# A window-attention block and a deformable convolution in one kernel: ScalarE's two-step work split within a slot, with semaphores of its own, and a tile's turns and matmul one slot later

## The chip, the cores and the metric

The kernel runs on one core of one Trainium2 chip. The metric is the device time of one execution in microseconds (us); smaller is better. The engines are TensorE (PE, its weight loads PEld), VectorE (DVE), ScalarE (ACT), GpSimd (POOL) and SyncE (SP), which issues the DMAs here. Each works through its own program in order and meets the others only at semaphores.

## The reference

The input is 16 images of 128 channels and 56x56 pixels. Two layers run one after the other. Cut to what matters:

```python
# layer 0, per image
x = x + dwconv3x3(x)
q, k, v = layernorm(x) @ qkv_w + qkv_b           # 7x7 windows of 8x8 pixels
idx = top_k(mean_q @ mean_k, 4)                   # each window picks 4 windows
o = softmax(q . k[idx] * scale) @ v[idx]          # 49 windows, 4 heads
x = x + (o + dwconv5x5(v)) @ wo                   # the 5x5 one is "lepe"
x = x + mlp(layernorm(x))                         # 128 -> 384, gelu, 384 -> 128
# layer 1, per image
off = relu(conv1x1([relu(conv1x1(gated x)), 2 * feat_up]))
dy, dx, m = conv3x3(off)                          # 8 groups x 9 taps = 72 samples a pixel
out = relu(sum over 72 samples of bilinear(feat_up at (y+dy, x+dx)) * sigmoid(m) @ w_dcn) + x
```

The bilinear sample is computed without a gather. Its weight in a row or a column is the hat max(0, 1 - |distance|), so a column hat times the map is a matmul, and the row hats are multiplied in and summed afterwards.

## The kernel before, in words

Work is cut into **slots**. An image has 28 tiles of two rows and 9 slots q = 0 to 8 in each tile, so 252 slots n. Every engine has a `body(xi, di)` that walks these 252 slots with two images at once: layer 0 of image `xi` and, beside it, the deformable part of the image before, `di`. `body(0, None)` opens, 15 bodies have both (one for image 1, 14 in a hardware loop), and `body(None, 15)` closes with the deformable part alone. In a slot, the order of the calls is the order in which the engine does the work; nothing reorders it.

**The deformable part in a slot.** PE computes `windows` (L956, 32 matmuls) from `hats` and `fx`; DVE multiplies by the row weights in `weigh` (L1473), two slots of PSUM banks ahead at most; POOL adds rows once in three slots (`add_rows`, L634, L636, L639). ACT turns the column distances that a DMA has spread over `hats` into hats, one quarter buffer in each slot and three slots ahead of the matmuls that use them: `column_hats` (L1165 to L1167) is Abs, a drain, then Relu of 1 - x. Once a tile come, for the tile two ahead: the 18 matmuls of `offsets` in slot 0 (L926), `outside` on ACT in slot 1 (L1177 to L1179), `turn_columns` on PE and `copy_columns` on ACT in slot 2 (L933, L1172), and the sigmoid of the masks, `masks`, on ACT in slot 3 (Exp, drain, Ln, drain, Exp, L1184 to L1188). For the tile one ahead ACT makes the row hats in slot `WYH` = 2 (`row_hats`, Abs, drain, Relu, L1193 to L1195). For the tile before, PE turns the samples in the slots `VT` = 3, 4, 6 (`turn_samples`, L969, which waits for POOL's `general`, L722), ACT copies each turn out in the same slot (`copy_samples`, L1200, into `valt`), and in slot `WD` = 7 PE does `deform`, the 18 matmuls of L977, and ACT the `relu` behind it (L1206). POOL's `finish` (L646) waits for that.

**Layer 0 in a slot.** `x_slot` (ACT, DVE) and `x_first` and `x_rest` (PE) hold it. Slots 0 to 26 do the 3x3 convolution on DVE, 9 to 51 the q, k, v projections, 59 to 205 the attention, 81 to 216 the projections and the MLP of the 7 bands (`post`, steps k = 0 to 9, one band every 21 slots), 225 to 238 the offset features. Attention has one window each three slots. In the first (q = 2, 5 or 8) PE computes `scores` (L848), DVE the maxima (L1390) and ACT two Exp (`exps`, L1117); in the second (q = 0, 3 or 6) PE turns the result (L857) and ACT copies it (`copy_turned`, L1123, tile `pt`); in the third (q = 1, 4 or 7) PE does `pv` (L865) and DVE scales the heads (L1397, L1403, tile `osb`). The next `scores` waits for that, because all of it shares one PSUM bank. DVE also has one or two of the 25 taps of `lepe` (L1418) in nearly every slot from 62 to 207, ahead of the scaling.

On ACT a slot is: `column_hats`; then `outside`, `copy_columns`, `row_hats`, `masks`, `copy_samples` or `relu` where the slot has one; then `x_slot`. On PE it is: `windows`, `x_first` (scores or pv), `offsets`, `turn_columns`, `turn_samples` or `deform`, then `x_rest` (the steps of `post` and, behind them, the turn of the scores).

Of the kernel before, what the change touches and what calls it, by code (L numbers as in the profile page):

```python
# [34 lines left out]
CP = 4  # L35
# [19 lines left out]
OM, PXT, VT, WD, WYH = 0, 2, (3, 4, 6), 7, 2  # L55
# [81 lines left out]
def build(nc, a, out):  # L137
# [9 lines left out]
    with ExitStack() as ctx:  # L147
# [162 lines left out]
        s_hb = [sem(f"columns_spread{s}") for s in range(HR)]  # L310
        s_hat = sem("column_hats_ready")
# [729 lines left out]
        def _(act):  # L1041
# [119 lines left out]

            def column_hats(i, n, c):
                act.wait_ge(s_hb[n % HR], cnt(i, 32 * NT * NG // HR, 32 * (n // HR + 1)))
                v = hats[:, n % HR, c * CP:(c + 1) * CP, :].rearrange("p j n -> p (j n)")
                act.activation(v, v, ACT.Abs, bias=const("xneg"))  # L1165
                act.drain()  # L1166
                act.activation(v, v, ACT.Relu, scale=-1.0, bias=1.0).then_inc(s_hat, 1)  # L1167
# [6 lines left out]
            def outside(i, t):  # L1174
                act.wait_ge(s_pxy, cnt(i, NT, t + 1))
                wait(act, s_fm, cnt(i, NT, t))
                act.activation(tmpf[:], pxy[t % 4][:, 0:S], ACT.Abs, bias=const("mid"))  # L1177
                act.drain()
                act.activation(tmpf[:], tmpf[:], ACT.Relu, bias=const("mid"), accum_out=vmx[:]).then_inc(s_vm, 1)  # L1179

            def masks(i, t):
                m = pxy[t % 4][:, 2 * S:3 * S]
                act.wait_ge(s_cl, cnt(i, NT, t + 1))
                act.activation(m, m, ACT.Exp, scale=-1.0)  # L1184
                act.drain()
                act.activation(m, m, ACT.Ln, bias=1.0)
                act.drain()
                act.activation(m, m, ACT.Exp, scale=-1.0).then_inc(s_msk, 1)  # L1188

            def row_hats(i, t):  # L1190
                v = wy[t % 2][:].rearrange("p s r -> p (s r)")
                act.wait_ge(s_wa, cnt(i, NT, t + 1))
                act.activation(v, v, ACT.Abs)  # L1193
                act.drain()
# [33 lines left out]
            def body(xi, di):  # L1228
                for t in range(NT):
# [4 lines left out]
                    for q in range(Q):  # L1234
                        hi, hg = group_of(di, xi, t * NG + q // CPG + 1)
                        if hi is not None:
                            column_hats(hi, hg, q % CPG)
# [318 lines left out]
```

## Time and profile before

| | us |
|---|---|
| median of 3 runs | 14506.09 |
| lowest and highest | 14485.17 and 14514.5 |
| the profiled execution | 14479.08 |
| its span, first to last instruction | 14477.3 |

The page of the profiled execution gives PE 78% of the span busy, ACT 66%, DVE 60%, POOL 48%. The mean granted TensorE clock is 0.896 of full speed. The bodies repeat: after a setup of some 1,080 us each of the 15 full bodies takes about 830 us, but one, which has in it one pass of the general path of `general` on POOL. The last body takes some 515 us. A profile is read here by stretches of one body, and within attention by the three slots of a window, since the shares over the whole span are means over stretches with different limits.

### The profile page before, as it was taken

Reading aid. Unit: us, or ns where it says so; the run is one execution under the profiler, and the core shown is the slowest. Engines: PE = TensorE matmul, PEld = TensorE weight load, DVE = VectorE, ACT = ScalarE, POOL = GpSimd, SP = SyncE. Lnnn points to the kernel's source line nnn. Section 1 sums busy time; section 2 is a strip of 40 time slices with the busy share of each in tenths; the row PEclk is TensorE's granted clock in tenths of the full one; section 3 lists DMA queues with packets and bytes.
Section 4 is the critical chain, followed back from the end, with each engine's and each line's share of the span. In section 5 each row is a group of like instructions: output and inputs, shape, how many; then the busy total and the mean of one; then the engine's idle time right before and its main releaser. Section 6 shows DMA issues by size and latency. Waiting matters only on the chain.

```text
span 14477.3 us, 470729 instructions
## 1 busy us (share of the span) xinstructions
PE 11349.7 (78%) x170988; PEld 8705.5 (60%) x170988; DVE 8630.8 (60%) x12547; ACT 9600.7 (66%) x20318; POOL 6951.3 (48%) x6167
## 2 busy tenths in 40 slices
PE   3568888888888888888888888888888888851887
PEld 2346666666666666666666666666666666641666
DVE  7436657566665756656665666566575666631743
ACT  1227777767777776777777777777777677751777
POOL 0005454545545454544545454454545454466467
PEclk9668999999999989999999999999899999975998
DMA  4214444444444444444444444444444444431444
GB/s 140 67 46 113 108 116 108 114 107 110 112 111 111 106 114 107 113 109 112 111 105 114 110 113 108 114 111 109 113 109 114 108 112 109 112 84 23 106 122 112
DMA packets 1848281, 1535.26 MB, mean 106 GB/s; under 512 B 1006880, under 2 KB 1382176, under 8 KB 1841760
## 3 DMA queue, kind: packets, MB, share of 16 engines
q1 hardware_dynamic: 1835776, 1494.30, 41.0%
q8 instruction: 1421, 23.28, 0.7%
q14 instruction: 1868, 15.30, 0.4%
q0 software_dynamic: 9216, 2.38, 0.2%
HBM read 1297.70 MB, written 198.21 MB: 103 GB/s over the span
## 4 chain that ended last, share of the span: by engine, by line
PE 36%; issue 15%; ACT 14%; ACTq 8%; DVE 7%; POOLq 6%; SPq 5%; DVEq 4%; POOL 4%; DMA 2%
ACTq L1166 6%; PE bank_small L926 6%; PE bank_small L977 5%; PE bank_scores L848 5%; PE windows L956 5%; PE bank_scores L865 4%; POOLq L635 3%; ACT hats L1165 3%; POOLq L637 2%; DVEq L1417 2%; POOL gbuf L706 2%; ACT pr L1117 2%; ACT hats L1167 2%; PE bank_turned L969 1%; PE bank_post L895 1%
## 5 line engine op out<-in xcount | busy, mean ns | idle before, releaser
L1473 DVE TENSOR_TENSOR prod<-windows,wy 128x640 f32<-128x640 f32 x4032 | 3278.2, 819 | 2680.0 <-PE windows L956 2640.0
L634 POOL TENSOR_TENSOR prod<-prod 128x768 f32<-128x768 f32 x1344 | 2462.6, 1832 | 2711.6 <-DVE prod L1473 2704.1
L956 PEld LDWEIGHTS windows<-fx,hats 64*64 64x64 f32 x129024 | 2721.5, 143 | 1367.7 <-issue 1298.2
L956 PE MATMUL windows<-fx,hats 64*64 64x80 f32 x129024 | 3341.0, 247 | 114.5 <-issue 105.3
L1165 ACT ACTIVATE hats<-hats,cst 128x512 f32<-128x512 f32 x4032 | 2877.8, 714 | 120.1 <-DMA hats<-sample_columns 84.3
L1418 DVE SCALAR_TENSOR_TENSOR ol<-xpad,lepw,ol 128x448 f32<-128x448 f32 x2688 | 2594.9, 965 | 236.0 <-issue 1.8
L1167 ACT ACTIVATE hats<-hats 128x512 f32<-128x512 f32 x4032 | 2541.7, 630 | 282.2 <-issue 10.4
L636 POOL TENSOR_TENSOR prod<-prod 128x384 f32<-128x384 f32 x1344 | 1580.6, 1176 | 212.3 <-issue 24.1
L926 PE MATMUL bank_small<-wom,ofp 128*128 128x216 f32 x8064 | 1627.9, 357 | 46.5 <-issue 46.5
L639 POOL TENSOR_TENSOR val<-prod 128x384 f32<-128x384 f32 x1344 | 1537.7, 1144 | 241.2 <-issue 159.9
L926 PEld LDWEIGHTS bank_small<-wom,ofp 128*128 128x128 f32 x8064 | 1470.5, 193 | 96.8 <-issue 52.7
L865 PE MATMUL bank_scores<-vsel,pt 128*128 128x64 f32 x6272 | 972.9, 304 | 706.4 <-ACT pt L1123 702.6
L969 PE MATMUL bank_turned<-cst,val 128*128 128x128 f32 x4032 | 826.3, 320 | 848.4 <-POOLq L722 616.4
L615 POOL TENSOR_SCALAR pxy<-pxy 128x72 f32<-128x72 f32 x448 | 179.0, 400 | 2620.0 <-DVE pxy L1458 1472.6
L848 PE MATMUL bank_scores<-ksel,qbd 128*128 128x256 f32 x3136 | 1072.3, 473 | 387.0 <-DVE osb L1403 319.5
L865 PEld LDWEIGHTS bank_scores<-vsel,pt 128*128 128x128 f32 x6272 | 857.7, 212 | 836.5 <-ACT pt L1123 808.2
L1117 ACT ACTIVATE pr<-bank_scores,nmx 128x256 f32<-128x256 f32 x1568 | 724.5, 466 | 944.5 <-DVE nmx L1390 944.4
L977 PE MATMUL bank_small<-valt,wdcn 128*128 128x128 f32 x8064 | 1070.4, 290 | 49.7 <-ACT valt L1200 48.8
L969 PEld LDWEIGHTS bank_turned<-cst,val 128*128 128x128 f32 x4032 | 497.4, 162 | 982.4 <-POOLq L722 651.2
L977 PEld LDWEIGHTS bank_small<-valt,wdcn 128*128 128x128 f32 x8064 | 998.7, 203 | 74.3 <-ACT valt L1200 60.7
L848 PEld LDWEIGHTS bank_scores<-ksel,qbd 128*128 128x128 f32 x3136 | 640.2, 226 | 570.3 <-issue 479.8
L646 POOL TENSOR_TENSOR xb<-xb,rt 128x112 f32<-128x112 f32 x448 | 192.8, 430 | 1495.1 <-ACT rt L1206 1493.2
(191 smaller groups left out, 13545.3 us busy)
## 6 DMA issues: line engine op xcount, KB each, us to landing
hats<-sample_columns SPq DMA_DIRECT2D x2688, 336.0 KB
ksel<-k_windows SPq DMA_DIRECT2D x3136, 32.0 KB
vsel<-v_windows SPq DMA_DIRECT2D x3136, 32.0 KB
fx<-map_columns SPq DMA_DIRECT2D x64, 420.0 KB
xpad<-in_x SPq DMA_DIRECT2D x17, 1568.0 KB, 14.1
map_columns<-fst SPq DMA_DIRECT2D x16, 1624.0 KB
feat_up<-fdense SPq DMA_DIRECT2D x16, 1568.0 KB, 14.1
q_windows<-qb SPq DMA_DIRECT2D x112, 224.0 KB, 2.7
```

The source lines that it names most:

```text
L634: pool.tensor_tensor(v[:, :, 0:n], v[:, :, 0:n], v[:, :, n:2 * n], ALU.add)
L636: pool.tensor_tensor(v[:, :, 0], v[:, :, 0], v[:, :, 1], ALU.add)
L639: pool.tensor_tensor(val[t % 2][:, g * GS * CG:(g + 1) * GS * CG].rearrange("p (s c) -> p s c", c=CG), v[:, :, 0], v[:, :, 2 if n == 3 els ...
L848: mm = pe.matmul(bs[:, h * 256:(h + 1) * 256], qbd[:, j, 2 * h:2 * h + 2, :].rearrange("p h q -> p (h q)"), ksel[s][:], start=True, stop=True)
L865: mm = pe.matmul(bs[:, h * W2:(h + 1) * W2], pt[:, h, m, :], vsel[w % NKV][:, m, h * W2:(h + 1) * W2], start=(m == 0), stop=(m == 1))
L926: mm = pe.matmul(bm[:, 0:3 * S], ofp[:, at:at + TP], wom[:, k, :], start=(k == 0), stop=(k == KK - 1))
L956: last[h] = pe.matmul(o[m], hat[:, m], fx[XP * h:XP * h + XP, g, row:row + WR, :].rearrange("p r c -> p (r c)"), start=True, stop=True)
L977: mm = pe.matmul(bm[:, 216:344], wdcn[:, k, :], valt[:, k, :], start=(k == 0), stop=(k == KK - 1))
L1165: act.activation(v, v, ACT.Abs, bias=const("xneg"))
L1167: act.activation(v, v, ACT.Relu, scale=-1.0, bias=1.0).then_inc(s_hat, 1)
L1418: dve.scalar_tensor_tensor(out=olv, in0=v, scalar=lepw[:, k:k + 1], in1=olv, op0=ALU.mult, op1=ALU.add)
L1473: dve.tensor_tensor(o, x, w.unsqueeze(3).to_broadcast([128, 2, CP * WR, CG]), ALU.mult).then_inc(s_wm, 1)
```

## The change

It has three parts.

1. **Own semaphores in place of drains, and the second step later in the slot.** `column_hats` is cut in two: `column_distances` (Abs, counts up `s_cab`) stays at the head of the slot, and `column_hats` (waits for `s_cab`, Relu) goes to its end, behind `x_slot`. `row_hats` is cut the same way (`row_sizes`, `s_rab`), and so is `outside` (`s_oab`, `outside_sum`); their second steps stand ahead of `x_slot` of the same slot. `masks` becomes three steps with `s_mst` between them: the first Exp in slot 3 where it was, the Ln at the end of slot 3, the last Exp at the end of slot 4.
2. **`VT` goes from (3, 4, 6) to (4, 5, 7)**: the turns of a tile's samples on PE and their copies on ACT are one slot later.
3. **`WD` goes from 7 to 8**: `deform` on PE and its `relu` on ACT are one slot later, and so share the slot with `scores` and `exps` where they shared it with `pv`.

```diff
-OM, PXT, VT, WD, WYH = 0, 2, (3, 4, 6), 7, 2
+OM, PXT, VT, WD, WYH = 0, 2, (4, 5, 7), 8, 2
...
+            def column_distances(i, n, c):
+                act.wait_ge(s_hb[n % HR], cnt(i, 32 * NT * NG // HR, 32 * (n // HR + 1)))
+                act.activation(chunk(n, c), chunk(n, c), ACT.Abs, bias=const("xneg")).then_inc(s_cab, 1)
+
             def column_hats(i, n, c):
-                act.wait_ge(s_hb[n % HR], cnt(i, 32 * NT * NG // HR, 32 * (n // HR + 1)))
-                v = hats[:, n % HR, c * CP:(c + 1) * CP, :].rearrange("p j n -> p (j n)")
-                act.activation(v, v, ACT.Abs, bias=const("xneg"))
-                act.drain()
-                act.activation(v, v, ACT.Relu, scale=-1.0, bias=1.0).then_inc(s_hat, 1)
+                act.wait_ge(s_cab, cnt(i, NT * Q, n * CPG + c + 1))
+                act.activation(chunk(n, c), chunk(n, c), ACT.Relu, scale=-1.0, bias=1.0).then_inc(s_hat, 1)
...
-            def masks(i, t):
+            def masks(i, t, step):
                 m = pxy[t % 4][:, 2 * S:3 * S]
-                act.wait_ge(s_cl, cnt(i, NT, t + 1))
-                act.activation(m, m, ACT.Exp, scale=-1.0)
-                act.drain()
-                act.activation(m, m, ACT.Ln, bias=1.0)
-                act.drain()
-                act.activation(m, m, ACT.Exp, scale=-1.0).then_inc(s_msk, 1)
+                if step == 0:
+                    act.wait_ge(s_cl, cnt(i, NT, t + 1))
+                    act.activation(m, m, ACT.Exp, scale=-1.0).then_inc(s_mst, 1)
+                elif step == 1:
+                    act.wait_ge(s_mst, cnt(i, 2 * NT, 2 * t + 1))
+                    act.activation(m, m, ACT.Ln, bias=1.0).then_inc(s_mst, 1)
+                else:
+                    act.wait_ge(s_mst, cnt(i, 2 * NT, 2 * t + 2))
+                    act.activation(m, m, ACT.Exp, scale=-1.0).then_inc(s_msk, 1)
...
                         if hi is not None:
-                            column_hats(hi, hg, q % CPG)
+                            column_distances(hi, hg, q % CPG)
                         if fi is not None and q == PXT - 1:
                             outside(fi, ft)
                         if fi is not None and q == PXT:
                             copy_columns(fi, ft)
                         if ni is not None and q == WYH:
-                            row_hats(ni, nt)
+                            row_sizes(ni, nt)
                         if fi is not None and q == PXT + 1:
-                            masks(fi, ft)
+                            masks(fi, ft, 0)
                         if pi is not None and q in VT:
                             copy_samples(pi, pt_, VT.index(q))
                         if pi is not None and q == WD:
                             relu(pi, pt_)
+                        if ni is not None and q == WYH:
+                            row_hats(ni, nt)
+                        if fi is not None and q == PXT - 1:
+                            outside_sum(fi, ft)
                         if xi is not None:
                             x_slot(xi, t * Q + q)
+                        if fi is not None and q in (PXT + 1, PXT + 2):
+                            masks(fi, ft, q - PXT)
+                        if hi is not None:
+                            column_hats(hi, hg, q % CPG)
```

## Rows read from the trace of the kernel before

**Rows 1.** The page's busy time of each engine, share of span, instructions.
```profile
PE 11349.7 (78%) x170988; PEld 8705.5 (60%) x170988; DVE 8630.8 (60%) x12547; ACT 9600.7 (66%) x20318; POOL 6951.3 (48%) x6167
```
**Rows 2.** Busy time by stretch: slots 27-58, 59-206 (most), 207-251 of one body; last body.
```profile
core 0: us, PE busy (x) PEld busy (x) DVE busy (x) ACT busy (x) POOL busy (x), PEclk, DMA share, GB/s
7818.00:7908.00 90.00, 77.60 (x1267) 56.67 (x1267) 39.65 (x61) 73.93 (x151) 50.09 (x46) 0.96 0.50 113
7992.00:8440.00 448.00, 375.04 (x5564) 294.78 (x5560) 313.64 (x495) 322.40 (x703) 205.78 (x182) 0.95 0.41 105
8440.00:8564.00 124.00, 103.62 (x1789) 76.26 (x1781) 50.00 (x69) 93.07 (x186) 73.23 (x69) 0.95 0.51 131
13970.00:14431.00 461.00, 371.65 (x8398) 319.76 (x8399) 191.33 (x275) 383.46 (x778) 345.54 (x326) 0.92 0.46 125
```
**Rows 3.** Waits over the whole execution: waiter, releaser, us in total, times, longest.
```profile
PE bank_scores L865 <- ACT pt L1123: 702.6, 542, 6.8
PE bank_turned L969 <- POOLq L722: 616.4, 94, 412.7
```
**Rows 4.** Timeline of ACT, slots 2 to 4 of a plain tile: start, us, instruction.
```profile
7206.43 0.20 ACT L1117 ACTIVATION_READ_ACCUMULATOR pr<-bank_scores,nmx 128x1 f32 x1
...
7209.02 0.59 ACT L1123 ACTIVATE pt<-bank_scores 128x512 f32<-128x512 f32 x1
7209.50 0.72 ACT L1165 ACTIVATE hats<-hats,cst 128x512 f32<-128x512 f32 x1
7210.29 0.63 ACT L1167 ACTIVATE hats<-hats 128x512 f32<-128x512 f32 x1
```
**Rows 5.** Timeline of PE and DVE, slots 2 to 5 of that tile; idle and releaser bracketed.
```profile
7203.17 1.10 PE L848 MATMUL bank_scores<-ksel,qbd 128*128 128x256 f32 x4 [0.66 <-DVE osb L1403]
...
7204.31 0.69 DVE L1390 TENSOR_REDUCE nmx<-bank_scores 128x2 f32<-128x512 f32 x1 [0.43 <-PE bank_scores L848]
...
7206.68 0.66 PE L857 MATMUL bank_scores<-cst,pr 128*128 128x128 f32 x4 [0.99 <-ACT pr L1117]
...
7209.66 1.23 PE L865 MATMUL bank_scores<-vsel,pt 128*128 128x64 f32 x8 [1.62 <-ACT pt L1123]
...
7211.39 0.46 DVE L1403 TENSOR_TENSOR osb<-bank_scores,rinv 64x64 f32<-64x64 f32 x2
...
7212.74 1.48 PE L848 MATMUL bank_scores<-ksel,qbd 128*128 128x256 f32 x3
```
**Rows 6.** Busy time in three stretches, each from a window's maxima to its scaled heads.
```profile
7204.31:7211.85 7.54, 4.93 (x97) 3.91 (x100) 7.09 (x11) 6.39 (x17) 4.58 (x4) 0.91 0.57 141
7214.48:7221.10 6.62, 5.17 (x94) 4.51 (x95) 6.18 (x10) 4.37 (x10) 3.50 (x3) 1.00 0.47 126
7223.43:7231.51 8.08, 7.10 (x126) 6.44 (x126) 7.64 (x11) 5.51 (x14) 5.27 (x5) 1.00 0.45 116
```
**Rows 7.** Timeline of PE and ACT, slots 7, 8, 0 and 2 behind it.
```profile
7218.45 1.10 PE L865 MATMUL bank_scores<-vsel,pt 128*128 128x64 f32 x8 [0.80 <-ACT pt L1123]
...
7219.39 2.23 PE L977 MATMUL bank_small<-valt,wdcn 128*128 128x128 f32 x18
...
7222.26 1.13 PE L848 MATMUL bank_scores<-ksel,qbd 128*128 128x256 f32 x4
...
7224.04 3.55 PE L926 MATMUL bank_small<-wom,ofp 128*128 128x216 f32 x18
...
7231.65 1.10 PE L848 MATMUL bank_scores<-ksel,qbd 128*128 128x256 f32 x4 [1.12 <-DVE osb L1403]
```
**Rows 8.** Timeline around slot 3 of a tile with a step of the MLP's norm.
```profile
8005.62 0.55 ACT L1129 ACTIVATE t<-bank_post 128x448 f32<-128x448 f32 x1
...
8009.87 0.63 DVE L1433 TENSOR_TENSOR yw<-t 128x448 f32<-128x448 f32 x1 [4.06 <-ACT t L1134]
```
**Rows 9.** Timeline of the last body: PE at slot 3, POOL at its third addition.
```profile
14209.21 0.55 PE L969 MATMUL bank_turned<-cst,val 128*128 128x128 f32 x3 [1.62 <-POOLq L722]
...
14220.27 1.82 POOL L634 TENSOR_TENSOR prod<-prod 128x768 f32<-128x768 f32 x1 [0.80 <-DVE prod L1473]
```

More of the change, by code:

```diff
@@ L310, in build @@
         s_hb = [sem(f"columns_spread{s}") for s in range(HR)]
+        s_cab = sem("column_distances_ready")
+        s_rab = sem("row_distance_sizes_ready")
+        s_oab = sem("outside_distances_ready")
+        s_mst = sem("mask_step_done")
         s_hat = sem("column_hats_ready")
@@ L1160, in offset_features, with chunk @@
                                    ACT.Relu).then_inc(s_of, 1)
-            def column_hats(i, n, c):
-                act.wait_ge(s_hb[n % HR], cnt(i, 32 * NT * NG // HR, 32 * (n // HR + 1)))
-                v = hats[:, n % HR, c * CP:(c + 1) * CP, :].rearrange("p j n -> p (j n)")
-                act.activation(v, v, ACT.Abs, bias=const("xneg"))
-                act.drain()
-                act.activation(v, v, ACT.Relu, scale=-1.0, bias=1.0).then_inc(s_hat, 1)
+            def chunk(n, c):
+                return hats[:, n % HR, c * CP:(c + 1) * CP, :].rearrange("p j n -> p (j n)")
+            def column_distances(i, n, c):
+                act.wait_ge(s_hb[n % HR], cnt(i, 32 * NT * NG // HR, 32 * (n // HR + 1)))
+                act.activation(chunk(n, c), chunk(n, c), ACT.Abs, bias=const("xneg")).then_inc(s_cab, 1)
+            def column_hats(i, n, c):
+                act.wait_ge(s_cab, cnt(i, NT * Q, n * CPG + c + 1))
+                act.activation(chunk(n, c), chunk(n, c), ACT.Relu, scale=-1.0, bias=1.0).then_inc(s_hat, 1)
             def copy_columns(i, t):
@@ L1176, in outside, with outside_sum, row_sizes @@
                 wait(act, s_fm, cnt(i, NT, t))
-                act.activation(tmpf[:], pxy[t % 4][:, 0:S], ACT.Abs, bias=const("mid"))
-                act.drain()
+                act.activation(tmpf[:], pxy[t % 4][:, 0:S], ACT.Abs, bias=const("mid")).then_inc(s_oab, 1)
+            def outside_sum(i, t):
+                act.wait_ge(s_oab, cnt(i, NT, t + 1))
                 act.activation(tmpf[:], tmpf[:], ACT.Relu, bias=const("mid"), accum_out=vmx[:]).then_inc(s_vm, 1)
-            def masks(i, t):
+            def masks(i, t, step):
                 m = pxy[t % 4][:, 2 * S:3 * S]
-                act.wait_ge(s_cl, cnt(i, NT, t + 1))
-                act.activation(m, m, ACT.Exp, scale=-1.0)
-                act.drain()
-                act.activation(m, m, ACT.Ln, bias=1.0)
-                act.drain()
-                act.activation(m, m, ACT.Exp, scale=-1.0).then_inc(s_msk, 1)
+                if step == 0:
[7 more added lines that the diff above has]
+                    act.activation(m, m, ACT.Exp, scale=-1.0).then_inc(s_msk, 1)
+            def row_sizes(i, t):
+                v = wy[t % 2][:].rearrange("p s r -> p (s r)")
+                act.wait_ge(s_wa, cnt(i, NT, t + 1))
+                act.activation(v, v, ACT.Abs).then_inc(s_rab, 1)
             def row_hats(i, t):
                 v = wy[t % 2][:].rearrange("p s r -> p (s r)")
-                act.wait_ge(s_wa, cnt(i, NT, t + 1))
-                act.activation(v, v, ACT.Abs)
-                act.drain()
+                act.wait_ge(s_rab, cnt(i, NT, t + 1))
                 act.activation(v, v, ACT.Relu, scale=-1.0, bias=1.0).then_inc(s_wh, 1)
```

## The prediction, made before the changed kernel was built

> **What bounds the kernel now.** I read the page's busy shares first: no engine is near its limit over the span, PE at 78% and ACT at 66% [rows 1]. So the bound has to be looked for in stretches. The busy time of the stretches of one body [rows 2] shows two kinds. In attention (448 us of 830) PE is busy 375 us, ACT 322 and DVE 314, nobody full. Around it, in slots 27 to 58 and 207 to 251, ACT has 74 of 90 us and 93 of 124 us and DVE well under half: there ACT is nearest to the bound. In the last body ACT is at 383 and POOL at 346 of 461 us.
>
> The waits say what stands between the engines in attention. The largest of PE on ACT is that of the pv matmuls for the copied turn, 702.6 us in 542 waits [rows 3]. The wait of the sample turns for POOL, 616.4 us, is 412.7 us of one single wait, the general path, and 204 us of 93 ordinary ones [rows 3].
>
> Then I followed one plain tile. A window runs in a circle: scores, maxima, exps, turn, copy, pv, scaling, next scores. From the scores of slot 2 (7203.17) to those of slot 5 (7212.74) it takes 9.57 us [rows 5], from there to those of slot 8 (7222.26) 9.52 and on to those of slot 2 (7231.65) 9.39 [rows 5, 7]. Two things share this time. In the PE/ACT part, the exps end at 7206.63 and the copy starts only at 7209.02, and pv stands idle 1.62 us for it [rows 4, 5]. And DVE, from the maxima to the scaled heads, is filled: 7.09 of 7.54 us, 6.18 of 6.62, 7.64 of 8.08, the rest being the drains between the taps [rows 6]. So two bounds lie close together, and what one part of the change frees the other may keep.
>
> **The change part by part.** The sum is made against the profiled execution, 14479.08 us (span 14477.3 and 1.8 around it). The median of the runs, 14506.09, lies 27 us above it; I add that at the end. A body has 148/9 = 16.4 tiles of attention, and 15 bodies have attention beside the deformable part.
>
> *What a drain costs.* Without a drain, the Abs of 7209.50 starts 0.11 us before the copy ahead of it ends (7209.02 + 0.59). With one, the Relu starts at 7210.29, 0.07 us after the Abs ends (7209.50 + 0.72) [rows 4]. A drain with other work to put in its place is 0.18 us. Where Abs and Relu still stand next to each other, the wait for the own semaphore takes the drain's place. No row shows such a wait; the nearest is a wait for another engine's semaphore: maxima 0.03 us after the scores end (7203.17 + 1.10 to 7204.31, 0.04) [rows 5]. I take it as equal to the drain's 0.07, with bounds from 0.03 less to 0.1 more each.
>
> *Slots 2 to 5.* Today 2.39 us lie between exps and copy: Abs, drain, Relu, the three mask steps, the copy of the samples [rows 4]. Afterwards it is the Relu of the exps' slot (0.63 - 0.11 = 0.52), the next Abs (0.61) and one Exp of the masks (some 0.16): 1.3 us, so 1.1 less, and pv's 1.62 falls to 0.5. What is late next is DVE: its stretch ends at 7211.85, so the scores can start at 7211.88 and not before, where they started at 7212.74 [rows 5, 6]. **Gain 0.86 us**. The sample turn that leaves slot 3 gains nothing there: it ran inside PE's wait for the exps, which grows by as much (0.99 to 1.5) [rows 5].
>
> *Slots 5 to 8.* `deform` (7219.39 to 7221.62) stands between pv and the next scores, while DVE has the heads at 7221.10 [rows 6, 7]. With `deform` gone and one sample turn (some 0.5 us) in its place, PE is ready before DVE, and the scores start at 7221.13 and not at 7222.26: **gain 1.13 us**. The cheaper copy of slot 6, which would take pv's idle 0.80 [rows 7], brings nothing on top, since DVE is the bound.
>
> *Slots 8 to 2.* `deform`'s 2.2 us now stand behind the scores of slot 8, and ahead of the windows of slot 0, of `offsets` (7224.04, 3.55 us) and of the turn [rows 7]. ACT's `relu` waits for it, and the exps queue behind the relu. That delay of the exps is covered: PE has `offsets` to do before it wants them. But PE's own work is serial, so the circle grows by 2.2 us, less what DVE gets ready meanwhile: of the 1.12 us in which scores wait for heads today [rows 7] I take half. **Loss 1.6 us**, bounds 1.0 and 2.2. Net of the three: -0.4 us a tile, -0.4 x 16.4 x 15 = **-100 us**. Bounds: -2.0 + 1.0 = -1.0 a tile (-250), and the loss alone with 1.6 (+390).
>
> *The MLP's steps.* With a norm in slot 3, DVE waits 4.06 us for ACT, whose last read of the PSUM bank had ended at 8006.17 [rows 8]: hats, masks and sample copy lie between, 1.2 us of which go behind. That is 3 of the 7 bands. In the others the norm gains 0.2 to 0.5, and each Gelu has only an Abs ahead of it, 0.8 earlier. Together 3.6 + 1.4 + 5.6 = 10.6 us a body; DVE waits in its queue with taps behind, so most passes. I take 8: **-120 us**, bounds 0 and -160.
>
> *The stretches that ACT holds.* 3.6 tiles in slots 27 to 58 and 5 in 207 to 251. Nine drains a tile get something in their place: 9 x 0.18 = 1.6 us, 14 us a body. With some of the 204 us of ordinary waits for POOL, which the later turn avoids, and with slots 0 to 26, where DVE's 3x3 taps bound, left out, I take 12: **-180 us**, bounds 0 and -250.
>
> *The clock.* In the attention stretch the granted clock is 0.95 [rows 2], so a tenth of it, 45 us, ran at 1.2 GHz and not at 2.4, behind the idle of slots 3 and 4: there pv takes 1.23 us against 1.10 and 3 of 4 score matmuls 1.48 against 1.10 for all four [rows 5, 7]. At most half, 22 us a body, comes back. The idle falls in slot 4 and grows in slots 3 and 8, so I take 5: **-75 us**.
>
> *The last body.* PE waits 1.62 us a tile for POOL in slot 3, but POOL has just 0.80 us idle before its third addition [rows 9] and is the bound. **-10 us** for 26 tiles, bounds 0 and -20.
>
> What is added and costs nothing: four counters more, and a wait of ACT per Relu. Behind the Relu's wait stands the next slot's Abs, and PE wants these hats three slots later. The mask's last Exp comes a slot later for POOL's use in the next tile. The copies of the samples are done in slot 7, and `deform` in 8 is the only one that wants them. `finish` on POOL waits one slot more, and POOL is half idle in attention (206 of 448 us) [rows 2].
>
> Sum: -100 - 120 - 180 - 75 - 10 = -485 us, so 13994 for the profiled execution and 14021, **about 14020 us**, for the median.
>
> **The rivals.**
>
> *Slower, by `deform` in the circle.* The mechanism is the loss of slots 8 to 2. It decides as soon as the two gains together stay under it, 1.6 us. Against: the rows show 0.86 and 1.13 us free behind DVE's stretches. For: DVE's stretches are 93 to 95% full, and POOL adds beside them for 3.5 to 5.3 us of each [rows 6]; if the reordering lengthens DVE's work, the gains are eaten. With no gain at all in the two links and none at the MLP's steps, +390 - 180 = +210: **14720 us**. Chance 0.11.
>
> *The own semaphores bring nothing.* If a wait for a count that ACT itself has just raised exposes as much as the drain, also where work stands between, the 180 us of the ACT stretches go, and the moved steps stay: 14020 + 180 = **14200 us**. Against: the Abs is long over when the Relu comes behind a copy. Chance 0.15. The Trainium skill (Perfetto Trace Analysis, DVE / Act Engine Instruction) says that an engine raises its semaphore only once its writes are acknowledged, and that the update then still has to propagate. By that, a wait right behind its producer is no cheaper than the drain; the trace of before has no such wait to agree or not.
>
> *The clock comes back whole.* If the idle that is left in slots 3 to 5 is too thin to bring the clock down, all 22 us a body return and not 5: 260 us more, **13760 us**. For: slot 4's wait, the longest, is the one that goes. Against: slots 3 and 8 get idler. Chance 0.12. The Trainium skill (TensorE: Matmul & The Clock Gate, Part 1) says that the gate goes by how busy PE has lately been, which would make less idle worth more than its own length.
>
> *Nothing changes.* DVE's circle bounds all the tile and takes back what the other stretches give: **14500 us**, chance 0.06.
>
> **How the numbers follow.** The forecast has 0.56. Its own terms, with their bounds (-250 to 0 around the tile, -160 to 0, -250 to 0), give 13880 to 14250. The range is to leave out no more than 2 in 10: it reaches down past 13760 to 13700, and up to 14400, where the own semaphores and half of the MLP's and the tile's gains fail together; 14720 is left out. Within 0.2% (about what a measurement of this kernel can tell from no change) is only the last rival: 0.06. Slower 0.11, faster 0.83.
>
> **What would show it.** The copy of the turn in slot 3 starts 1.3 us behind the exps, and PE's wait for it, 702.6 us, falls under 300. The scores of slots 5 and 8 follow the heads at once: PE's wait for `osb` grows. From the scores of slot 8 to those of slot 2 it is near 11 us. The turn of the samples no longer waits for POOL but for the one general path. ACT's gaps of 0.07 us before the Relu are gone in slots with work. The granted clock rises a little. The prediction is wrong if DVE's stretches from maxima to heads get longer, or if they start earlier than their taps allow me to think, since the DVE bound carries both gains.

## The result and the profile after

The changed kernel takes 14060.47 us (median of 4 runs, 14037.43 to 14078.87), the kernel before, run beside it, 14501.42 us (median of 4, 14485.17 to 14514.5). The ratio is 0.9696, 95% interval 0.9677 to 0.9715: 3.0% faster, where the forecast was 14020 us, some 3.4% below the 14506 us that it started from. The profiled execution took 14078.87 us with a span of 14077.1, 400 us less than that of before. In what follows, lines of the changed kernel have other numbers: L852 scores, L861 turn, L869 pv, L973 turn of the samples, L981 `deform`, L1121 exps, L1127 copy (`pt`), L1171 and L1175 the Abs and Relu of the column hats, L1427 the scaled heads, L1497 the row weights.

The page's busy times, to be held against [rows 1]: ACT's busy time has gone down by 516 us with the same 20318 instructions. Nearly all of it is overlap, since time that two records share counts once: the durations themselves add up to 10724 us before and to 10712 us after. Of the column hats' 4032 Relus none started before the end of the instruction ahead of it, and now 3771 do, by 0.10 us each. With drains in the new places ACT's busy time is 9568.9 us, close to the 9600.7 us of before.

```profile
PE 11000.8 (78%) x170988; PEld 8551.4 (61%) x170988; DVE 8501.4 (60%) x12547; ACT 9084.8 (65%) x20318; POOL 6883.1 (49%) x6167
```

The stretches of [rows 2] in the same body: slots 27 to 58, 81 to 206, 207 to 250, and the last body. Columns as there; the one ahead of the DMA share is the granted clock.

```profile
core 0: us, PE busy (x) PEld busy (x) DVE busy (x) ACT busy (x) POOL busy (x), PEclk, DMA share, GB/s
7591.00:7674.40 83.40, 76.30 (x1300) 55.97 (x1299) 38.91 (x60) 66.72 (x145) 47.75 (x45) 1.00 0.54 122
7761.70:8192.30 430.60, 359.80 (x5569) 287.76 (x5568) 307.71 (x494) 306.80 (x704) 203.19 (x182) 0.98 0.43 109
8192.30:8302.70 110.40, 98.80 (x1711) 72.75 (x1710) 45.71 (x67) 84.72 (x180) 66.01 (x63) 0.95 0.56 142
13588.00:14039.00 451.00, 371.80 (x8462) 318.73 (x8454) 192.09 (x276) 360.49 (x774) 345.00 (x327) 0.94 0.47 127
```

All four are shorter (the third is one slot shorter than its row in [rows 2], too), and the granted clock is higher in all but the third. As a mean of 13 bodies, from the first window matmul of a slot to that of another, in us:

| slots | before | after | ScalarE's part alone (act_only) |
|---|---|---|---|
| 0-26 | 83.6 | 86.8 | 82.7 |
| 27-58 | 90.5 | 83.4 | 85.4 |
| 59-80 | 84.1 | 85.6 | 84.3 |
| 81-206 | 448.6 | 432.1 | 428.6 |
| 207-250 | 119.6 | 111.0 | 115.0 |
| last body | 515.1 | 498.7 | 490.8 |

The plain tile of [rows 4 to 7], in the same body and slots, ACT first: from the exps of slot 2 to the copy of slot 3.

```profile
7001.45 0.20 ACT L1121 ACTIVATION_READ_ACCUMULATOR pr<-bank_scores,nmx 128x1 f32 x1
7001.54 0.62 ACT L1175 ACTIVATE hats<-hats 128x512 f32<-128x512 f32 x1
7002.06 0.71 ACT L1171 ACTIVATE hats<-hats,cst 128x512 f32<-128x512 f32 x1
7002.68 0.25 ACT L1195 ACTIVATE pxy<-pxy 128x72 f32<-128x72 f32 x1
7002.83 0.58 ACT L1127 ACTIVATE pt<-bank_scores 128x512 f32<-128x512 f32 x1
```

The copy comes 1.18 us behind the exps, where [rows 4] has 2.39. PE's and DVE's timeline of that tile, from the scores of slot 2 to those of the next slot 2 (idle and releaser in brackets):

```profile
6998.23 1.10 PE L852 MATMUL bank_scores<-ksel,qbd 128*128 128x256 f32 x4 [1.34 <-DVE osb L1427]
...
7003.47 1.10 PE L869 MATMUL bank_scores<-vsel,pt 128*128 128x64 f32 x8 [0.40 <-ACT pt L1127]
...
7006.46 0.46 DVE L1427 TENSOR_TENSOR osb<-bank_scores,rinv 64x64 f32<-64x64 f32 x2
...
7007.06 1.10 PE L852 MATMUL bank_scores<-ksel,qbd 128*128 128x256 f32 x4 [1.45 <-DVE osb L1427]
...
7015.28 1.10 PE L852 MATMUL bank_scores<-ksel,qbd 128*128 128x256 f32 x4 [1.51 <-DVE osb L1427]
...
7016.22 2.17 PE L981 MATMUL bank_small<-valt,wdcn 128*128 128x128 f32 x18
...
7018.43 0.37 ACT L1222 ACTIVATE rt<-bank_small,cols 128x128 f32<-128x128 f32 x1 [3.72 <-PE bank_small L981]
...
7026.19 1.10 PE L852 MATMUL bank_scores<-ksel,qbd 128*128 128x256 f32 x4 [0.66 <-DVE osb L1427]
```

The three circles take 8.83, 8.22 and 10.91 us, against 9.57, 9.52 and 9.39 [rows 5, 7]. Both shorter ones end in a wait of 1.5 us for DVE's heads, and the third has `deform` in it. pv, which took 1.23 us in [rows 5], and the scores of slot 5, three of which took 1.48 us there, take 1.10 us again. DVE's three stretches, from the maxima to the heads, as in [rows 6]:

```profile
6999.37:7006.92 7.55, 4.43 (x114) 3.57 (x113) 7.11 (x11) 6.89 (x18) 4.59 (x4) 1.00 0.58 154
7008.20:7015.14 6.94, 4.53 (x114) 3.54 (x112) 6.49 (x10) 5.78 (x13) 3.82 (x3) 1.00 0.48 131
7016.42:7026.04 9.62, 9.11 (x144) 8.32 (x142) 6.75 (x11) 5.36 (x15) 5.18 (x5) 1.00 0.39 106
```

The first two are full (7.11 of 7.55 us, 6.49 of 6.94). In the third PE is: 9.11 of 9.62. The waits over the whole execution (waiter, releaser, us in total, times, longest), beside [rows 3]:

```profile
PE bank_scores L869 <- ACT pt L1127: 727.3, 478, 413.7
PE bank_scores L852 <- DVE osb L1427: 588.4, 683, 2.6
ACT valt L1216 <- PE bank_turned L973: 722.6, 777, 8.4
ACT pr L1121 <- DVE nmx L1414: 250.8, 45, 18.5
```

The general path's 413 us now stand in front of pv, one slot on, so that pv's ordinary waits are 313.6 us, not 702.6. The waits of ACT for the maxima have nearly gone (944.4 us before), and ACT waits for the turn of the samples instead.

### The profile page after: what moved, and what is told of

Its sections match the earlier page's. It is cut to its first block, busy times and chain, and to the rows that moved or that the text cites. A ratio compares the mean times of both kernels' runs of the same rounds, so it can differ in the third digit from the quotient of the medians.

```text
span 14077.1 us, 469161 instructions
## 1 busy us (share of the span) xinstructions
PE 11000.8 (78%) x170988; PEld 8551.4 (61%) x170988; DVE 8501.4 (60%) x12547; ACT 9084.8 (65%) x20318; POOL 6883.1 (49%) x6167
## 4 chain that ended last, share of the span: by engine, by line
PE 38%; issue 15%; ACT 13%; DVEq 10%; DVE 9%; SPq 6%; POOL 4%; POOLq 3%; DMA 2%; ACTq 1%
PE bank_small L930 8%; PE windows L960 6%; DVEq L1441 6%; PE bank_small L981 6%; PE bank_scores L852 5%; ACT hats L1171 3%; DVE ol L1442 3%; ACT hats L1175 2%; DVEq L1422 2%; PE bank_scores L869 2%; POOL gbuf L710 2%; SPq L492 2%; PE bank_post L903 2%; POOLq L639 2%; PE bank_turned L973 1%
## 5 line engine op out<-in xcount | busy, mean ns | idle before, releaser
L1497 DVE TENSOR_TENSOR prod<-windows,wy 128x640 f32<-128x640 f32 x4032 | 3293.4, 820 | 1927.1 <-PE windows L960 1803.6
L960 PEld LDWEIGHTS windows<-fx,hats 64*64 64x64 f32 x129024 | 2652.3, 139 | 1391.6 <-issue 1322.9
L960 PE MATMUL windows<-fx,hats 64*64 64x80 f32 x129024 | 3283.9, 243 | 240.8 <-issue 201.6
L1171 ACT ACTIVATE hats<-hats,cst 128x512 f32<-128x512 f32 x4032 | 2877.1, 714 | 162.2 <-DMA hats<-sample_columns 101.5
L1442 DVE SCALAR_TENSOR_TENSOR ol<-xpad,lepw,ol 128x448 f32<-128x448 f32 x2688 | 2464.0, 917 | 236.1 <-issue 1.8
L1175 ACT ACTIVATE hats<-hats 128x512 f32<-128x512 f32 x4032 | 2513.8, 623 | 6.7
L643 POOL TENSOR_TENSOR val<-prod 128x384 f32<-128x384 f32 x1344 | 1502.5, 1118 | 241.2 <-issue 156.0
L852 PE MATMUL bank_scores<-ksel,qbd 128*128 128x256 f32 x3136 | 989.2, 443 | 723.9 <-DVE osb L1427 588.4
L869 PE MATMUL bank_scores<-vsel,pt 128*128 128x64 f32 x6272 | 941.5, 297 | 738.1 <-ACT pt L1127 727.3
L869 PEld LDWEIGHTS bank_scores<-vsel,pt 128*128 128x128 f32 x6272 | 828.9, 206 | 868.8 <-ACT pt L1127 839.4
L852 PEld LDWEIGHTS bank_scores<-ksel,qbd 128*128 128x128 f32 x3136 | 596.4, 211 | 901.0 <-issue 799.7
L1216 ACT ACTIVATE valt<-bank_turned 128x384 f32<-128x384 f32 x1344 | 652.2, 485 | 722.7 <-PE bank_turned L973 722.6
L981 PE MATMUL bank_small<-valt,wdcn 128*128 128x128 f32 x8064 | 1053.3, 288 | 54.4 <-ACT valt L1216 47.5
L981 PEld LDWEIGHTS bank_small<-valt,wdcn 128*128 128x128 f32 x8064 | 1015.2, 202 | 97.6 <-ACT valt L1216 58.2
L1414 DVE TENSOR_REDUCE nmx<-bank_scores 128x2 f32<-128x512 f32 x784 | 542.6, 692 | 612.2 <-PE bank_scores L852 612.2
L1121 ACT ACTIVATE pr<-bank_scores,nmx 128x256 f32<-128x256 f32 x1568 | 722.7, 467 | 250.9 <-DVE nmx L1414 250.8
```

Of the source, the lines that this page charges most:

```text
L643: pool.tensor_tensor(val[t % 2][:, g * GS * CG:(g + 1) * GS * CG].rearrange("p (s c) -> p s c", c=CG), v[:, :, 0], v[:, :, 2 if n == 3 els ...
L852: mm = pe.matmul(bs[:, h * 256:(h + 1) * 256], qbd[:, j, 2 * h:2 * h + 2, :].rearrange("p h q -> p (h q)"), ksel[s][:], start=True, stop=True)
L869: mm = pe.matmul(bs[:, h * W2:(h + 1) * W2], pt[:, h, m, :], vsel[w % NKV][:, m, h * W2:(h + 1) * W2], start=(m == 0), stop=(m == 1))
L960: last[h] = pe.matmul(o[m], hat[:, m], fx[XP * h:XP * h + XP, g, row:row + WR, :].rearrange("p r c -> p (r c)"), start=True, stop=True)
L981: mm = pe.matmul(bm[:, 216:344], wdcn[:, k, :], valt[:, k, :], start=(k == 0), stop=(k == KK - 1))
L1171: act.activation(chunk(n, c), chunk(n, c), ACT.Abs, bias=const("xneg")).then_inc(s_cab, 1)
```

## The experiments

All ratios are to the kernel before, run on the same chip. The means over 13 bodies of the three circles of attention, in us, in plain tiles (no step of the MLP's chain near) and in the others:

| kernel | ratio | plain: 2-5, 5-8, 8-2 | others: 2-5, 5-8, 8-2 |
|---|---|---|---|
| before | 1 | 9.57, 9.73, 9.38 | 11.49, 11.46, 11.81 |
| changed | 0.9696 | 8.99, 8.44, 10.95 | 9.92, 9.45, 13.57 |
| act_only | 0.9659 | 9.00, 9.01, 9.38 | 10.08, 11.38, 11.76 |
| moves_only | 0.9977 | 9.34, 8.47, 10.91 | 10.86, 9.65, 13.53 |
| sem_in_place | 0.9909 | 9.54, 9.57, 9.38 | 11.07, 11.39, 11.77 |
| relu_before_x | 0.9859 | 9.74, 8.51, 11.04 | 10.38, 10.19, 13.52 |
| deform_7 | 0.9697 | 8.97, 9.04, 9.39 | 9.92, 11.42, 11.77 |
| split_7_8 | 0.9649 | 9.36, 8.69, 9.59 | 9.97, 10.81, 12.26 |
| split_4_5_7 | 0.9580 | 9.57, 8.44, 9.11 | 10.67, 10.50, 11.72 |
| before_13_taps | - | 9.55, 9.74, 8.93 | 11.47, 11.41, 11.66 |
| after_13_taps | - | 8.08, 7.46, 10.93 | 9.63, 9.96, 13.44 |

**Each part alone.** The changed kernel with the old slots:

```diff
-OM, PXT, VT, WD, WYH = 0, 2, (4, 5, 7), 8, 2
+OM, PXT, VT, WD, WYH = 0, 2, (3, 4, 6), 7, 2
```

> ScalarE's part of the change alone: the turns of the samples stay in slots 3, 4, 6 and the deformable matmuls in slot 7. My theory, that ScalarE's reordering carries the gain and the move of the deformable matmuls costs about what it gives: slots 2 to 5 gain some 0.6 us a tile, slots 5 to 8 some 0.7, slots 8 to 2 nothing, with the MLP's steps, the ScalarE-held stretches and some clock about 0.957 of the time before, between 0.950 and 0.970. Rival, that the later turns and matmuls carry it: above 0.980.

Measured: 13994.64 us, 0.9659 (0.9643 to 0.9675), inside the range, not at its 0.957, and faster than the changed kernel. The circle of slots 8 to 2 is as before. The gain of slots 2 to 5 is the whole one; slots 5 to 8 gain 0.7 in plain tiles and almost nothing in the others. In the plain tile of the rows one sees what still holds this circle: the heads are there as `deform` ends, and the scores are late not for DVE but for PE's own work, `deform` and the windows behind it (act_only, same tile):

```profile
6988.94 2.23 PE L981 MATMUL bank_small<-valt,wdcn 128*128 128x128 f32 x18
...
6990.68 0.46 DVE L1427 TENSOR_TENSOR osb<-bank_scores,rinv 64x64 f32<-64x64 f32 x2
...
6991.81 1.13 PE L852 MATMUL bank_scores<-ksel,qbd 128*128 128x256 f32 x4
```

The other part is the kernel before with `VT = (4, 5, 7)` and `WD = 8`, the same line the other way round:

> The turns in slots 4, 5, 7 and the deformable matmuls in slot 8 alone, with ScalarE's order and drains as before. My theory: slots 2 to 5 gain up to 0.5 us a tile, slots 5 to 8 1.1, slots 8 to 2 lose 1.6 or more: 0.995, between 0.985 and 1.010. Rival, that the moves carry the gain: below 0.980.

Measured: 14451.53 us, 0.9977 (0.9967 to 0.9987). The move gives 1.3 us in slots 5 to 8 and takes 1.5 in slots 8 to 2 of a plain tile. Outside attention it also costs: 87.7 against 83.6 us in slots 0 to 26, and 553.4 against 515.1 in the last body. In the last body POOL's `finish` now waits for the relu, which comes a slot later. These are the waits there in the kernel before (13941 to 14456 us), moves_only (13876 to 14429) and the changed kernel (13555 to 14054):

```profile
POOL xb L646 <- ACT rt L1206: 5.8, 9, 1.2
```
```profile
POOL xb L646 <- ACT rt L1206: 82.5, 28, 4.0
```
```profile
POOL xb L650 <- ACT rt L1222: 29.3, 27, 2.5
```

In slots 0 to 26 the same wait grows from 0.2 to 5.5 us a body (4.8 in the changed kernel). It comes with the longer time; no run takes it out by itself.

The two parts' gains, 3.4% and 0.2%, would add up to 3.6%, and both together give 3.0%: with ScalarE's part in place, the move takes 0.4% back.

**Drain or own semaphore.** In the kernel before, at each of the places, for instance:

```diff
-                act.activation(v, v, ACT.Abs, bias=const("xneg"))
-                act.drain()
+                act.activation(v, v, ACT.Abs, bias=const("xneg")).then_inc(s_cab, 1)
+                act.wait_ge(s_cab, cnt(i, NT * Q, n * CPG + c + 1))
```

> Each drain of the column hats, row hats, outside distances and masks becomes a wait for ScalarE's own semaphore, at the place where the drain was, nothing else. My theory, that such a wait right behind its producer exposes what the drain did: 1.000, between 0.997 and 1.003. Rival, that the drain itself is dear (0.07 us gap and 0.11 us of overlap lost, over 4032 column hats): 0.985 or lower.

Measured: 14350.89 us, 0.9909 (0.9893 to 0.9926), between the theory and its rival and outside of both. The wait is not the drain's equal: it is cheaper, where the prediction had argued that it can't be. The gap between Abs and Relu is 0.032 us as the median of all 4032 (0.04 in these rounded lines), and 0.068 with the drain (0.07 in [rows 4]):

```profile
7121.33 0.70 ACT L1169 ACTIVATE hats<-hats,cst 128x512 f32<-128x512 f32 x1
7122.07 0.63 ACT L1171 ACTIVATE hats<-hats 128x512 f32<-128x512 f32 x1
```

Then the changed kernel with drains in the new places:

```diff
-                act.wait_ge(s_cab, cnt(i, NT * Q, n * CPG + c + 1))
+                act.drain()
```

and the same for `s_oab`, `s_rab` and both waits for `s_mst`.

> The changed kernel with its new order on ScalarE and its later turns, but each wait for ScalarE's own semaphore is a drain again. My theory, that a drain costs 0.18 us where other work stands between and that this is worth some 12 us a body outside attention: 0.982 of the time before, between 0.976 and 0.988. Rival, that only the order counts: 0.970 as the changed kernel. Rival, that a drain at the end of a slot is worse than before, since it waits for the copy or exps just issued: above 0.990.

Measured: 14322.09 us, 0.9887 (0.9871 to 0.9904), just past the upper end of the range, 0.988. So of the 3.0%, 1.9% hang on the semaphores, some 277 us. The 180 in the sum were for the stretches that ACT holds alone. There the changed kernel is 5.7 and 4.1 us a body shorter than this one, some 150 us in all; 44 us more are in the last body (542.4 against 498.7), where the sum had 10 for everything, and 2.7 us a body in slots 81 to 206. The groups of ACT say it for the Relu of the column hats alone (busy us, mean ns, idle before it): the last number is 282.2 us in the kernel before. These are sem_in_place, order_with_drains and the changed kernel, in this order:

```profile
L1171 ACT ACTIVATE hats<-hats 128x512 f32<-128x512 f32 x4032 | 2541.9, 630 | 127.8
```
```profile
L1175 ACT ACTIVATE hats<-hats 128x512 f32<-128x512 f32 x4032 | 2548.4, 632 | 339.0 <-issue 19.5
```
```profile
L1175 ACT ACTIVATE hats<-hats 128x512 f32<-128x512 f32 x4032 | 2513.8, 623 | 6.7
```

In the changed kernel 3771 of the 4032 Relus start 0.10 us before the instruction ahead of them has ended; with drains they start 0.08 us after it (both are medians). That is 0.18 us each, as worked out ahead, and 0.7 ms of ACT's time over the 3771; by the ratios, all drains together were worth 0.28 ms at the end.

**The place of the Relu.** The changed kernel with the call ahead of layer 0's work:

```diff
+                        if hi is not None:
+                            column_hats(hi, hg, q % CPG)
                         if xi is not None:
                             x_slot(xi, t * Q + q)
...
-                        if hi is not None:
-                            column_hats(hi, hg, q % CPG)
```

> The changed kernel with the Relu of the column hats ahead of the exps and copies of layer 0 and not behind them; the own semaphores and the rest stay. My theory: between exps and the copy of the turn lie one Relu and one Abs either way, so attention stays; only where nothing else stands between Abs and Relu 0.13 us are exposed again: 0.973 of the time before, between 0.970 and 0.979. Rival, the place behind layer 0's work is what counts: above 0.980.

Measured: 14283.44 us, 0.9859 (0.9840 to 0.9878). The rival holds. I had counted what lies between exps and copy, one Relu and one Abs either way, and not what lies ahead of the exps. The same slots 2 to 4 of that kernel:

```profile
7090.50 0.61 ACT L1175 ACTIVATE hats<-hats 128x512 f32<-128x512 f32 x1
7091.02 0.45 ACT L1121 ACTIVATE pr<-bank_scores,nmx 128x256 f32<-128x256 f32 x1
...
7092.66 1.19 PE L960 MATMUL windows<-fx,hats 64*64 64x80 f32 x32
...
7093.84 1.97 PE L869 MATMUL bank_scores<-vsel,pt 128*128 128x64 f32 x8
```

The exps start 2.94 us after the scores (7088.08), in the changed kernel 2.41 (6998.23 to 7000.64). Behind the exps the Relu runs beside the turn on PE, which has to come anyway; ahead of them it is on the path. And behind that longer idle PE falls to the lower clock: it is granted 1.00 until 7092 us, with 1.95 us of idle just before the turn, and 0.50 from 7094 on. pv takes 1.97 us and not 1.10, and the mean granted clock is 0.903 and not 0.919. All of the loss is in attention: slots 81 to 206 take 446.8 us and not 432.1, while slots 27 to 58 and 207 to 250 stay at 83.4 and 111.2, so the exposed 0.13 us that I expected there cost nothing.

**Where `deform` stands.** `VT, WD = (4, 5, 6), 7` in the changed kernel:

> The changed kernel with the deformable matmuls back in slot 7; for that the turns of the samples are in slots 4, 5, 6. My theory, that these matmuls in slot 8 lengthen slots 8 to 2 by 1.9 us a tile and shorten slots 5 to 8 by 1.4, and meet the 18 matmuls of the offsets in the next slot outside attention: as ScalarE's part alone, 0.966 of the time before, between 0.962 and 0.969, with the circles at about 9.5, 11.0 and 10.5 us. Rival, that it is the turns one slot later that cost: 0.970 or more.

Measured: 14051.16 us, 0.9697 (0.9681 to 0.9713), and not 0.966: just outside the range, and by its mechanism the rival. In attention it is like act_only in every circle. What it loses against it, it loses elsewhere: 85.5 against 82.7 us in slots 0 to 26, 505.9 against 490.8 in the last body. So there it is the later turns of the samples that cost. In its last body PE's turns wait 44.2 us for ACT's copies of the samples (`valt`), and 2.8 us in act_only; in slots 0 to 26 this wait is under 1 us a body in both, and no run shows what costs there.

The two kernels that cut `deform`'s 18 matmuls, the first on the changed kernel, the second also with `VT = (3, 4, 6)` and the relu in slot 7:

```diff
-            def deform(i, t):
-                pe.wait_ge(s_ve, cnt(i, NG * NT, NG * t + NG))
+            def deform(i, t, k0=0, k1=KK):
+                pe.wait_ge(s_ve, cnt(i, NG * NT, NG * t + k1 // 3))
...
-                for k in range(KK):
+                for k in range(k0, k1):
...
-                        if pi is not None and q == WD:
-                            deform(pi, pt_)
+                        if pi is not None and q in PARTS:
+                            deform(pi, pt_, *PARTS[q])
...
+PARTS = {7: (0, 6), 8: (6, 9)}                  # split_7_8
+PARTS = {4: (0, 3), 5: (3, 6), 7: (6, 9)}       # split_4_5_7
```

> The changed kernel with the deformable matmuls cut in two: 12 of 18 in slot 7, behind pv, where TensorE waits for the heads, 6 in slot 8. My theory: slots 8 to 2 get 1.2 us shorter than in the changed kernel, slots 5 to 8 some 0.5 longer, 0.7 us a tile: 0.960 of the time before, between 0.954 and 0.966. Rival, that VectorE is the bound in all three circles: 0.970, as the changed kernel.

Measured: 13970.58 us, 0.9649 (0.9633 to 0.9665). The time is inside the range. Slots 8 to 2 of plain tiles get 1.36 us shorter than in the changed kernel; slots 5 to 8 get 0.25 longer in plain tiles and 1.36 in the others, and slots 2 to 5, which the forecast left alone, 0.37 longer in plain tiles.

> ScalarE's part with the turns back in slots 3, 4, 6, and the deformable matmuls cut in three: 6 each in slots 4, 5 and 7, all behind pv or scores, where TensorE waits anyway. My theory: slots 5 to 8 fall from 10.9 to 9.8 us, the others stay: 0.951 of the time before, between 0.945 and 0.960. Rival, VectorE bounds the tile: 0.966, as ScalarE's part alone.

Measured: 13870.3 us, **0.9580 (0.9564 to 0.9596)**, the fastest of all that compute the reference's output, inside the range though not at its 0.951: against act_only slots 5 to 8 do fall to 8.44 us in plain tiles, but slots 2 to 5 rise from 9.00 to 9.57, so the third of `deform` in slot 4 isn't covered, and the last body rises from 490.8 to 508.0.

**Whether DVE bounds the circles.** Both kernels with fewer taps of `lepe`, 13 kept of the 25 and 12 left out:

```diff
-            return b, range(25 * j // last, 25 * (j + 1) // last)
+            return b, range(13 * j // last, 13 * (j + 1) // last)
```

> The kernel before with 13 of the 25 taps of the 5x5 convolution left out or not done (12 fewer a band on VectorE), so its output is not the reference's. It asks which circle VectorE bounds. My theory: slots 2 to 5 fall by 0.5 us at most (from 10.6), slots 5 to 8 stay near 11.2, since the deformable matmuls bound them, slots 8 to 2 fall by up to 0.9: 0.975 to 0.990 of the time before. Rival, VectorE bounds nothing: all three circles within 0.1.

> The changed kernel with the same 12 taps a band left out; its output is not the reference's. My theory: slots 2 to 5 and 5 to 8, which VectorE bounds there, fall by 0.6 us each (from 9.5), slots 8 to 2, bound by TensorE, by 0.3 at most: 15 to 25 us a body more than the changed kernel gains, 0.942 to 0.958 of the time before. Rival, VectorE bounds nothing there: 0.968.

Measured: 0.9638 and 0.9324 (13968.27 and 13512.48 us). These times can't be set against the expectations as they are. With other values in x, the general path isn't taken at all: its indirect DMAs are absent from both traces, and with them some 410 us of one body. The circles of the table aren't touched by that, nor are the bodies without the general path, and by these both expectations were too high: slots 0 to 250 of a body get 6.6 us shorter in the kernel before (826.3 to 819.7), where 0.975 to 0.990 meant 10 to 24, and 10.4 in the changed one (798.9 to 788.5), where 15 to 25 was expected. In the plain tiles of the kernel before, 12 taps less change slots 2 to 5 and 5 to 8 by 0.02 us: DVE is not the bound there. In those of the changed kernel they take 0.91 and 0.98 us off: it is. Slots 8 to 2 are the other way round, 0.45 us before and 0.02 after. In the tiles with the MLP's steps of the changed kernel the fewer taps take 0.3 us off slots 2 to 5, and slots 5 to 8 get 0.5 us longer; there DVE isn't the bound.

**The clock by itself.** In the kernel before, matmuls into columns of a window bank that nobody reads:

```diff
+            def filler(i, n, k):
+                wait(pe, s_wm, cnt(i, NT * Q, n))
+                for j in range(k):
+                    pe.matmul(hb[(n + 1) % 2][:, j % 2, 320:448], ident, ident, start=True, stop=True)
```

> The kernel before with work put into TensorE's waits: 5 matmuls of 128x128 in slot 3 and 8 in slot 4 of attention, into unused columns of a PSUM bank, results not read. If the clock matters by itself: the granted clock rises from 0.90 to 0.92 or more and the time falls by 0.2 to 0.8% though there is more work. Rival, that the slow stretches lie where TensorE waits anyway: the clock rises and the time stays or grows, 1.000 to 1.010.

Measured: 14389.01 us, 0.9934 (0.9918 to 0.9951), with a granted clock of 0.919. PE does more, waits less and is done 0.7% sooner. Here the Trainium skill (TensorE: Matmul & The Clock Gate, Part 1), which has the clock follow PE's own recent activity, agrees with the run: matmuls in PE's waits, and nothing else in the edit, went with a granted clock up from 0.896 to 0.919. In slots 81 to 206, where they stand, PE ran 10 us of a body at 1.2 GHz and not 47, and the stretch got 4.6 us shorter (448.6 to 444.0). The same on split_4_5_7, with 5 and 4 in attention and 8 in slot 3 elsewhere:

> The kernel with the deformable matmuls in slots 4, 5 and 7 (0.958) with idle-time matmuls put in: in attention 5 in slot 3 and 4 in slot 4, elsewhere and in the last body 8 in slot 3, where TensorE waits for GpSimd at half the clock. If the clock is worth its own time: granted clock from 0.920 to 0.935 or more and 0.950 to 0.956. Rival, the matmuls put in fill time that is now needed: 0.960 or more.

Measured: 13933.68 us, 0.9610 (0.9590 to 0.9629), at a granted clock of 0.938, the highest of all and no gain: the rival. Its last body ran at 0.94 where split_4_5_7's ran at 0.88, and took 518.5 us and not 508.0. One tile of it (L990 is the filler, L974 the turn):

```profile
13603.21 0.78 PE L961 MATMUL windows<-fx,hats 64*64 64x80 f32 x32
...
13603.93 2.05 PE L990 MATMUL windows<-cst 128*128 128x128 f32 x16
...
13605.80 0.39 POOL L620 TENSOR_SCALAR pxy<-pxy 128x72 f32<-128x72 f32 x1 [2.46 <-issue]
13605.81 0.49 PE L974 MATMUL bank_turned<-cst,val 128*128 128x128 f32 x3
13606.15 1.83 POOL L639 TENSOR_TENSOR prod<-prod 128x768 f32<-128x768 f32 x1
```

The filler fills PE's wait to its end, and the turn still starts 2.60 us behind the windows (13603.21), as it did in split_4_5_7 (2.64, with 1.86 us of idle for POOL's `general`, L727). POOL, 2.46 us of whose time go by there without a wait that the profile shows, then goes on at once with its addition. So a faster PE has nobody to hurry at this place. That this is why the clock brought nothing is my reading of one tile, and what made the last body longer is not shown.

## Why the prediction was right, and where it wasn't

**The bound.** That attention has two bounds close together, PE with ACT and DVE, was right, and the runs with 13 taps show it more sharply than the rows could: before, DVE bounds neither slots 2 to 5 nor 5 to 8; after, it bounds both, in plain tiles.

**Slots 2 to 5, 5 to 8, 8 to 2.** Forecast for the plain tile -0.86, -1.13 and +1.6 us; in the tile of the rows -0.74, -1.30 and +1.52, over all plain tiles -0.58, -1.29 and +1.57. The net, -0.4, is -0.3 us. The copy's 1.3 us behind the exps is 1.18, pv's 0.5 us of idle is 0.40.

**The MLP's steps** were put at 8 us a body. Over the other tiles the three circles sum to 32.94 us and not 34.76, 1.8 us less each, much more than in plain ones (0.3). With 8 or so such tiles a body, that is nearly all of the 15.0 us by which slots 59 to 206 shrink (532.7 to 517.7). The norm of [rows 8], in the same slot: DVE waits 2.80 us and not 4.06, the 1.2 forecast.

```profile
7778.77 0.63 DVE L1457 TENSOR_TENSOR yw<-t 128x448 f32<-128x448 f32 x1 [2.80 <-ACT t L1138]
```

Taken as the surplus of these tiles over plain ones, 1.5 us each, the term was too small (12 us a body, not 8), and the terms around it too large: tile, steps and clock together were 20 us a body, and 15.0 came. But the surplus isn't ScalarE's alone. By itself ScalarE's part takes 1.3 us off a plain tile and 1.5 off the others (28.68 to 27.39 and 34.76 to 33.22), a surplus of 0.25, some 2 us a body. On top of it the move costs a plain tile 1.0 us and saves the others 0.3. How much of the surplus the steps' shorter waits carry stays open. Slots 8 to 2 cost 1.8 us more in these tiles than before (13.57 against 11.81), 0.2 more than forecast.

**A drain's price** was right at 0.18 us where work stands between. What was wrong is the line that a wait right behind its producer equals the drain: it is 0.04 us cheaper, which lies just beyond the bound of 0.03 less that I gave it, and over all places that alone is 0.9% (sem_in_place). The stretches held by ScalarE gained 7.1 and 8.6 us, where 12 for both was forecast; ScalarE's part alone gains 5.1 and 4.6 of it, and the move adds the rest. Slots 0 to 26, which I had left out as bound by DVE, lost 3.2: ScalarE's part gains 0.9 there, and the move costs 4.1. The rival that the own semaphores bring nothing is out: they carry 277 us.

**The clock** was put at 5 us a body, 75 us. The mean granted clock rose from 0.896 to 0.919, just what the filler does in the kernel before, and the filler is worth 0.66%, some 95 us, though it adds work. By the granted clock, PE's time at 1.2 GHz in slots 81 to 206 of a body fell from 47 us, the 45 of the forecast, to 21. So the size of the term is borne out as far as the two kernels compare; how much the clock is worth in the changed kernel itself, no run shows. The rival that all of it comes back is out, since almost half of these 47 us is left.

**The last body** gained 16 us, not 10, within its bounds of 20, and that was luck. The sum had PE's shorter wait for POOL bring it. That wait did shrink (56.6 to 18.9 us), but the move costs the last body time, 38 us alone (515.1 to 553.4) and 8 with ScalarE's part (490.8 to 498.7), and ScalarE's part, for which the sum had nothing there, gains 24.

**What was to cost nothing.** That `finish` waits one slot more was put at nothing, since POOL is half idle in attention. In the last body and in slots 0 to 26 it isn't nothing by the traces: the wait grows from 5.8 to 29.3 us and by some 4.5 us a body, where the move costs 8 us and 4.1 a body. That one makes the other is likely and not isolated.

**The rival of `deform` in the circle** has its mechanism shown: 1.5 us a tile (moves_only, 9.38 to 10.91). It didn't decide, since the gains of the other two circles passed it. But act_only shows what the forecast didn't see: the move, which I had counted as a gain of 1.13 and a loss of 1.6, costs 0.4% of the whole once ScalarE's part is in (0.9659 against 0.9696). Part of that lies outside attention, where the sum had the later turn as a gain (deform_7 against act_only), and the rest in plain tiles: with ScalarE's part in, slots 5 to 8 gain only 0.57 by it, since DVE bounds them at 8.44, and slots 8 to 2 lose 1.57.

**Of what would show it**: the wait of pv for the copy was to fall under 300 us and is 313.6. PE's wait for the heads grew, from 319.5 us in 374 waits to 588.4 in 683. The turn of the samples waits for ACT (82.9 us) or a little for POOL (42.8), and the general path shows at pv. DVE's stretches, which were not to get longer, are 7.55, 6.94 and 9.62 us against 7.54, 6.62 and 8.08; the third is held by PE, and the second by itself, 0.3 us longer, did not eat the gain. ACT's gaps before the Relu are gone where other work stands between, and the clock rose.

**The sum.** That 14060 lies within 0.3% of 14020 owes much to luck. Of the profiled executions' 400 us, where the sum had 485, the 15 bodies' attention gives some 225 us and not 295, the stretches that ACT holds 236 and not 180, slots 0 to 26 cost 48 and not nothing, slot 251 some 20, and the last body gives 16 and not 10. The errors have both signs and part of them cancel; the kernel before also ran 4.7 us faster beside the changed one than the median from which the forecast started. The range was less sure than it looked, too: the terms' own bounds, added straight, give 13760 to 14420 and not 13880 to 14250.

## What to carry to other kernels

Work of an in-order engine that belongs to another chain goes behind the instruction that a third engine waits for, and not ahead of it; there it runs under that engine's answer (relu_before_x against the changed kernel, 1.6%). On ScalarE, a drain between two dependent instructions is better a counter that the first one raises, and most of all with something independent put between. A block of matmuls is worth cutting where each piece fits a wait of PE (split_4_5_7), and before a step is moved to uncover one bound, ask with a run that has less of the other engine's work whether that one is next. A step that moves for one stretch's sake is in every stretch: look what it does where another engine holds the time (`finish`, in the last body).

## What was not expected of the hardware

A wait of ScalarE for a count that its own previous instruction raises leaves a gap of 0.03 us (sem_in_place), a drain 0.07 to 0.08 us (before, order_with_drains), and independent instructions overlap by 0.10 us (changed kernel). Idle that costs nothing in its own slot can cost in the next: 13 matmuls a tile put into PE's waits made the kernel 0.66% faster, with the granted clock up from 0.896 to 0.919, while the same idea on split_4_5_7, at 0.938, gave nothing.
